# Attention steps moved ahead of the sorted experts' blocks they stand beside

## The reference, cut to what is computed

```python
xn = layernorm(x)
# attention: 8 heads from latent projections (32 wide), keys and queries with a rotary part
scores = einsum('bhsd,bhtd->bhst', q, k) * scale
o = einsum('bhst,bhtd->bhsd', softmax(scores), v_c)
attn = o.reshape(b, s, 8 * 128) @ W_O + b_O
# experts: each token takes 2 of 8, with weights from its router scores
for e in range(8):
    h = silu(xn @ w_gate[e].T) * (xn @ w_up[e].T)
    ffn = ffn + dense_w[:, e:e + 1] * (h @ w_down[e].T)
x = x + attn + ffn
```

## Time and profile before

| what | us |
|---|---|
| median of 3 runs | 2679.3 (2676.52 to 2686.96) |
| the profiled execution, its own time | 2676.29 |
| its span, first to last instruction | 2674.3 |
| TensorE busy in the span | 2462.1 |
| VectorE busy | 2073.9 |
| ScalarE busy | 1632.9 |
| mean granted clock of TensorE | 0.967 |

### The profile page before, as it was taken

How to read it: one execution, slowest core, us unless ns; L and a number is a source line. 1 busy time by engine, 2 the same in 40 slices (tenths; PEclk the granted TensorE clock), 3 DMA queues, 4 the chain that set the end, 5 groups by cost and what they waited for, 6 DMA issues and landing times.

```text
span 2674.3 us, 67343 instructions
## 1 busy us (share of the span) xinstructions
PE 2462.1 (92%) x26752; PEld 1795.2 (67%) x26752; DVE 2073.9 (78%) x3553; ACT 1632.9 (61%) x2872; POOL 724.6 (27%) x601
## 2 busy tenths in 40 slices
PE   4989999999999999999988999899998999999998
PEld 2767657776666766667656676676765767667765
DVE  4958878688777887778876778768788687885976
ACT  2757457565566656666566655667456575575845
POOL 1211342204322052220522215212152122520235
PEclk8999999999999999999999999999899999999999
DMA  6110211102111031110211112011121111211022
GB/s 237 41 33 10 88 55 41 40 3 103 40 40 40 3 107 37 40 40 29 87 30 44 36 42 79 29 44 32 45 75 32 45 29 61 68 31 46 21 72 63
DMA packets 93370, 136.25 MB, mean 51 GB/s; under 512 B 10111, under 2 KB 55240, under 8 KB 92552
## 3 DMA queue, kind: packets, MB, share of 16 engines
q1 hardware_dynamic: 84872, 115.16, 13.3%
q0 software_dynamic: 8192, 16.79, 2.1%
HBM read 101.31 MB, written 30.61 MB: 49 GB/s over the span
## 4 chain that ended last, share of the span: by engine, by line
PE 57%; DVE 21%; issue 14%; ACT 6%; POOL 2%; DVEq 0%; ACTq 0%; POOLq 0%
PE ps L1399 9%; PE ps L1537 7%; DVE neg_max L1061 7%; PE ps L1477 6%; PE ps L1577 5%; DVE probsT L1076 5%; PE ps L1406 4%; ACT probs L722 4%; PE ps L1562 4%; PE ps L1628 4%; PE ps L1499 3%; PE ps L1420 2%; DVE ffn L1204 2%; PE ps L1372 2%; PE ps L1488 1%
## 5 line engine op out<-in xcount | busy, mean ns | idle before, releaser
L722 ACT ACTIVATE probs<-ps,neg_max 128x1024 f32<-128x1024 f32 x512 | 571.2, 1116 | 156.8 <-DVE neg_max L1061 155.1
L1061 DVE TENSOR_REDUCE neg_max<-ps 128x1 f32<-128x1024 f32 x512 | 624.6, 1220 | 31.6 <-PE ps L1537 20.6
L1537 PE MATMUL ps<-keys,q_parts 64*128 64x512 f32 x3072 | 505.0, 433 | 39.2 <-ACT probs L722 37.0
L1399 PE MATMUL ps<-q_parts,w_split 128*128 128x512 f32 x1536 | 467.0, 440 | 17.3 <-ACT ffn L771 9.6
L1562 PEld LDWEIGHTS ps<-ident,probs 64*128 64x128 f32 x8192 | 339.7, 140 | 122.8 <-ACT probs L722 52.7
L620 POOL TENSOR_TENSOR probs<-ffn,q_parts 128x512 f32<-128x512 f32 x208 | 297.3, 1432 | 382.7 <-DMA q_parts<-gate_rows 149.7
L1399 PEld LDWEIGHTS ps<-q_parts,w_split 128*128 128x128 f32 x1536 | 286.8, 192 | 164.3 <-issue 62.8
L1562 PE MATMUL ps<-ident,probs 64*128 64x64 f32 x8192 | 345.8, 224 | 41.6 <-ACT probs L722 35.5
L1537 PEld LDWEIGHTS ps<-keys,q_parts 64*128 64x128 f32 x3072 | 256.9, 189 | 181.0 <-ACT probs L722 86.2
L1076 DVE COPY probsT<-ps 128x512 f32<-128x512 f32 x512 | 350.4, 684 | 20.6 <-PE ps L1562 18.9
L1577 PE MATMUL ps<-probsT,latent 128*32 128x128 f32 x8192 | 332.1, 282 | 27.5 <-DVE o_latent L1054 21.3
(11 more groups left out here) (217 smaller groups left out, 3334.0 us busy)
## 6 DMA issues: line engine op xcount, KB each, us to landing
w_split<-w_parts SPq DMA_DIRECT2D x132, 256.0 KB, 2.6
q_parts<-gate_rows SPq DMA_DIRECT2D x64, 512.0 KB, 3.9
y_rows<-probs SPq DMA_DIRECT2D x40, 256.0 KB, 2.2
x_in<-in_x SPq DMA_DIRECT2D x9, 512.0 KB, 4.3
w_parts<-q_parts SPq DMA_DIRECT2D x2, 2048.0 KB, 13.7
out<-x_mid SPq DMA_DIRECT2D x8, 512.0 KB, 3.2
ffn<-in_gate_up SPq DMA_DIRECT2D x1, 2048.0 KB, 8.9
probsT<-in_gate_up SPq DMA_DIRECT2D x1, 2048.0 KB, 13.1
```

The costliest lines, as they stand in the source:

```text
L722: nc.scalar.activation(probs[:, t % 3, :], banks(2 * (t % 2)), ACT.Exp, bias=neg_max[:, t % 4:t % 4 + 1], accum_out=row_sum[:, g % 2, t % ...
L1061: nc.vector.tensor_reduce(neg_max[:, t % 4:t % 4 + 1], banks(2 * (t % 2)), X, ALU.max, negate=True).then_inc(max_ready.sem, 1)
L1399: mm = nc.tensor.matmul(ps[:, bank, :], w_split[:, f % CHUNK_SLOTS, h, k * P:(k + 1) * P], tokens[:, half], start=(part == 0), stop=(part ...
L1537: mm = nc.tensor.matmul(ps[:, 2 * (t % 2) + c, :], q_parts[rows, j, q, n * P:(n + 1) * P], keys[rows, k, :], start=(part == 0), stop=(part ...
```

## The change

On all three engines the call of the attention step moves from the end of iteration j of the block loop to its front, ahead of `gate_up(j)` on TensorE, of the silu of block j on ScalarE, and of the product of block j on VectorE. On VectorE the call for j = 0 thereby also comes ahead of `tokens_low(0)`. On TensorE `tokens(0)` stays ahead of the loop. The queries of the second run's first head, which were issued at the end of iteration `BLOCKS + 1`, are issued at the front of iteration `BLOCKS + 2`.

```diff
--- ScalarE
                 tokens_high(0)
                 for j in range(BLOCKS + BLOCK_DOWN_LAG):
+                    if QUAD_STEPS + T_LAG + j < PERIOD:
+                        attention_step(QUAD_STEPS + T_LAG + j)
                     if j < BLOCKS:
...
                         tokens_high(j // 4 + 1)
-                    if QUAD_STEPS + T_LAG + j < PERIOD:
-                        attention_step(QUAD_STEPS + T_LAG + j)
--- VectorE
-                tokens_low(0)
                 for j in range(BLOCKS + BLOCK_DOWN_LAG + 1):
+                    if QUAD_STEPS + T_LAG + j < PERIOD:
+                        attention_step(QUAD_STEPS + T_LAG + j)
+                    if j == 0:
+                        tokens_low(0)
                     if j < BLOCKS:
...
                         outputs(i // 4)
-                    if QUAD_STEPS + T_LAG + j < PERIOD:
-                        attention_step(QUAD_STEPS + T_LAG + j)
--- TensorE
                 for j in range(BLOCKS + BLOCK_DOWN_LAG):
+                    beside(j)
                     if j < BLOCKS:
                         first[j] = pe.value_load(...)
                         gate_up(j)
...
                         down(j - BLOCK_DOWN_LAG)
-                    beside(j)
...
                 def attention_tail(j):
-                    if j == BLOCKS + 1:
+                    if j == BLOCKS + 2:
                         queries(QUAD)
                     if QUAD_STEPS + T_LAG + j < PERIOD:
                         attention_step(QUAD_STEPS + T_LAG + j)
```

## The result

The changed kernel took 2652.8 us in the median of four runs (2648.49 to 2656.24), beside 2683.1 for the kernel before in four runs (2676.52 to 2687.11). The medians are 30.3 us apart; the ratio is 0.9893, with a 95% interval of 0.9865 to 0.992, which makes it 28.7 us less, between 21 and 36. The forecast was 2651, in a range of 2642 to 2666. It was made from three of the four runs before, with a median of 2679.3.

What follows compares the result with a forecast made beforehand. It took TensorE, busy 92% of the span, as the bound, with two holes and clock falls in each block phase. Gains of 11.0, 6.2 and 10.6 us made 27.8, from 2679.3 to 2651 us, range 2642 to 2666.

Steps and rivals of the forecast that it cites:

- The chain of waits: Block phase head: the scaling, its input ready, stood behind a product needing the first gate-up; TensorE waited 1.22 us.
- the wait for the scaling: First gate-up to first `values` call goes from 2.19 to 0.81 us: 1.38 x 8 = 11.0 us gained.
- V0 under the first hole: First `values` call of group 7 runs inside TensorE's 1.49 us wait before the first gate-up: 6.2 us gained.
- the later steps, a turn straight to a gate-up: Block loop on TensorE: distance taken as 0.62 us, bounds 0.31 and 0.62; gain 27.8 us, 30.3 with the other.
- the clock: First to fifth gate-up: TensorE's clock no longer falls; 10.57 us against 9.24 at full clock, 10.6 us gained.
- a comparison of two stretches: TensorE busy 1.79 of 3.50 us before a clock fall, 2.63 where it held; the change gives 2.44.
- (a): Rival: the block phase's clock falls as before, so only 17.2 us are gained: 2662 us; chance 0.18.
- (b): Rival: first `values` call not hidden before the first gate-up, clock falls too; 11.0 us gained, 2668; chance 0.06.
- (c): Rival: slower, clock falls in router and last experts lose 28.8 us against 17.2 gained: 2691; chance 0.04.
- the prediction's own sign for (c): Fifth gate-up comes 7.1 us after the first, and the span still isn't 28 us shorter.
- (d): Rival: TensorE stays blocked at the same places, so the edit does not do what it says: 2679; chance 0.02.

Runs made afterwards that it cites:

- experiment 1: The kernel before with only VectorE's scaling of group 6 moved ahead of `tokens_low(0)`: 2664.8 us, ratio 0.9958.
- experiment 4: The kernel before, nothing moved, with unread 128x512 matmuls, four in TensorE's 1.49 us hole and five in its 1.22 us hole: 2669.6 us, ratio 0.9951.
- experiment 2: As experiment 1 against the kernel before, with TensorE's first `values` call also moved ahead of the first gate-up: 2653.9 us, ratio 0.9922.
- the last pair: The changed kernel a third time and experiment 5 once more, side by side on one chip: 2653.9 and 2647.3 us.
- 6: The kernel before with four unread matmuls in TensorE's first hole (1.49 us) alone: 2670.9 us, ratio 0.9961.
- 7: The kernel before with five unread matmuls in TensorE's second hole (1.22 us) alone: 2672.1 us, ratio 0.9963.
- experiment 5: The changed kernel with two `values` calls ahead of the first gate-up, the later two one iteration earlier: 2643.5 us, again 2647.3.

## Why the prediction was right

**The chain of waits.** It went as read from the earlier trace rows: the scaling had its input early and stood behind a product that needed the first gate-up. The prediction had `values` start at the end of the transposes, 0.64 us after their start; it did (143.54 to 144.18). The other two moved operations cost nothing, as reckoned: ScalarE's copy of group 7's scale (L710, 151.56) runs before the silu it was put ahead of, which then still waits 0.64 us for its gate-up, and no product is late (one wait for a product at a gate-up in the whole launch, 0.4 us). The `values` calls' waits for the scaling came to 11.4 us, for about 11.5 forecast.

**The three terms**, against the runs, in us of the eight stretches:

| term | forecast | measured | by |
|---|---|---|---|
| the wait for the scaling | 11.0 | 10.8 | experiment 1's full-clock stretches against 4's |
| V0 under the first hole | 6.2 | 5.2 | (7.81 - 7.15) x 8, experiment 1 against 2 |
| the later steps, a turn straight to a gate-up | 0 (2.5 as the other bound) | 2.1 | experiment 2 against the changed kernel |
| the clock | 10.6 | 11.3 | experiment 4 against before |
| sum | 27.8 | 29.4 | 84.52 - 55.12 |

The measured terms add up to 29.4 by the way they are made, each a difference between two runs; the first two are drawn from the four stretches of experiment 1 that held the clock.

The mis-sized term is the turn straight to a gate-up. I took 0.62 us of the bounds 0.31 and 0.62, as if the load of the expert's register were added there; it measured 0.35, near the other bound. That is 0.27 x 8 = 2.2 us. Three other distances were off too, in the mean of eight: the first gate-up to V1 is 0.90 for 0.81 and tokens to `values` 0.53 for 0.43, while U to a gate-up is 0.39 for 0.49. These nearly cancel.

The split of the forecast has a slip that its sum does not show. The old stretch at full clock was put at 7.09 + 1.38 + 0.77 = 9.24, with the 0.62 of a turn straight to a gate-up in it. The old order has a turn to `values` in that place, 0.31; by the forecast's own distances it comes to 8.93. The clock's term would have been (10.57 - 8.93) x 8 = 13.1 and that of the later steps a loss of 2.5, with the same 27.8 in all. Experiment 4 measured 9.16. So that 10.6 lies so near to 11.3 is luck in part.

**The clock.** The term rested on a comparison of two stretches, and the experiments bear the term out: with the holes busy the clock holds, without moving anything. The argument for it was too narrow. It weighed the first hole alone, in the fourth sequence, the only one of before where the clock's record has the fall begin ahead of the second hole (0.8 us behind the first gate-up's start; 1.2 to 1.8 us in five sequences, 2.5 and 2.9 in two). The first hole alone did it in 6 of 16 sequences and the second in 1 of 8. What the change did was to shorten the one and remove the other, and that was enough in every sequence; that it would be, the two stretches could not tell. The Trainium skill, "TensorE: Matmul & The Clock Gate", section "A second HAM failure mode: psum-queue depth-cycling", describes a kernel in which frequent micro-idles between matmul groups make the clock swing between its levels. Of this the runs here show both sides: holes of 1.49 and 1.22 us in succession did it 16 times in 16, and the small ones that stay (0.68, 0.22 and 0.83 in succession) did not in 32.

**The rivals.** (a) would show granted clocks of 0.7 to 0.85 in the stretches; they are 1.00. (b) would show the gate-up later than 2.11 us behind the tokens; it comes after 2.12. (c), falls elsewhere, is real, and its size changes from one execution to the next. Behind the first tokens and outside the stretches the three profiles of the changed kernel took 3.0, 6.0 and 16.0 us more than the one of before; those of the experiments from 6.8 less to 6.4 more. That the clock is the cause of each was not tested. By the letter the prediction's own sign for (c) was met in the profiled pair: the stretches were as short as forecast and the spans only 20.1 us apart, not 28. One pair of executions cannot carry such a sign. (d): the moved order is in the timeline.

**To the end.** That the gain carries through the launch held within that: 26.4 of 29.4 us in the profile, and 6.6 us of stretches became 6.7 us of time in the last pair. Against the kernel before it is less exact. The changed kernel's medians are 30.3, 25.1 and 26.0 us lower, with stretches 29.4, 29.1 and 29.3 shorter. Experiments 1 and 2 gained less time than stretches (10.9 for 17.0, 21.8 for 27.3), experiments 4, 6 and 7 a little more (13.9 for 11.3, 12.6 for 10.3, 11.5 for 9.3). That the forecast of 2651 came within 2 us of the median is better than this spread allows, and luck in part.

## What to carry to other kernels

Where an engine waits for a short operation of another, look at what that operation's input waited for: if it had been ready for microseconds, the queue's order is the wait, and moving one instruction ahead can cost nothing, as here, where the engine stood waiting anyway. Such a hole is worth more than its length when TensorE's clock falls behind it; here 18 us of waits and small steps carried 11 us of clock with them. After a hole is partly filled, measure what is left of it, and move the next independent piece in.

## What the runs showed of the hardware that was not expected

Adding work can shorten a kernel. Nine matmuls of 128x512 in each block phase, whose results nobody reads, took 0.5% off, because TensorE's granted clock stayed at 1.00 where it had been at half for part of each stretch. The fall is not a matter of one hole: 1.49 us alone brought it in 6 of 16 sequences, 1.22 us alone in 1 of 8, the two with 0.97 us of matmuls between them in 16 of 16. And the register load ahead of a gate-up has no fixed price in the distances: a turn is followed by a gate-up after 0.22 to 0.51 us (experiment 5 and the changed kernel), and by `values`, which loads no register, after 0.31. Behind another gate-up the distance was 1.03 to 1.20 us (experiment 2), where tokens follow a gate-up after 0.80 and `values` after 0.90. No run takes the load out, so what it costs by itself is not shown.
